# Two reordered parts, one later load, two wide zero products and one more split block in a vision tower kernel

## What is computed

```python
h = tok(x)                      # 768-long patches @ W_lin.T + b, class token, positions
h = h + attn(layernorm(h))      # 16 heads of 64, relative position bias, w_o
h = h + ffn(layernorm(h))       # below
h = h + recurrence(layernorm(h))
h = h + channel_mix(layernorm(h))

def ffn(x):                     # 592 tokens, hidden 1024
    logits = x @ router_w.T     # 7 routed experts, the best 2 of a token
    top_w = softmax(top_k(logits, 2))
    mixed = sum_e combine[:, e] * swiglu(x, w_gate[e], w_up[e], w_down[e])
    return mixed + swiglu(x, sw_gate, sw_up, sw_down)      # one shared expert
# swiglu(x) = (silu(x @ wg) * (x @ wu)) @ wd
```

## Time and profile before

| | |
|---|---|
| median of 3 runs | 306.15 us (306.04 to 307.07) |
| the profiled execution | 306.31 us |
| its span, first to last instruction | 304.5 us |
| PE busy | 296.6 us, 97% |
| ACT, DVE, POOL busy | 186.2, 188.9, 154.8 us |
| data moved | 46.49 MB, 153 GB/s |

### The profile page before, as it was taken

One profiled execution on the slowest core, in us unless ns is written; L12 is line 12 of the kernel. 1 busy time (PEld: TensorE's weight loads), 2 busy tenths in 40 slices (PEclk: granted clock), 3 DMA queues, 4 the chain that ended last, 5 costly groups with the idle time before them and its releaser, 6 DMA issues.

```text
span 304.5 us, 7355 instructions
## 1 busy us (share of the span) xinstructions
PE 296.6 (97%) x3072; PEld 276.6 (91%) x3072; DVE 188.9 (62%) x365; ACT 186.2 (61%) x324; POOL 154.8 (51%) x142
## 2 busy tenths in 40 slices
PE   8999999999999999989999999999999999998995
PEld 7778889998999999989999999999999999985673
DVE  1694446575727868665818784756648686736962
ACT  3486346766546884656777575657576563668561
POOL 7042624665415151829576694957685775000333
PEclk9999999999999999999999999999999999999999
DMA  7969444463504222477765848383857562000002
GB/s 257 409 165 231 88 116 135 139 187 102 166 10 145 77 107 84 163 219 272 250 196 186 244 130 272 102 297 111 276 169 257 188 191 66 11 2 2 1 0 84
DMA packets 32464, 46.49 MB, mean 153 GB/s; under 512 B 6997, under 2 KB 18869, under 8 KB 32426
## 3 DMA queue, kind: packets, MB, share of 16 engines
q1 hardware_dynamic: 30026, 42.16, 44.3%
q0 software_dynamic: 960, 2.43, 2.4%
q10 hardware_dynamic: 1440, 1.38, 1.5%
HBM read 38.22 MB, written 5.71 MB: 144 GB/s over the span
## 4 chain that ended last, share of the span: by engine, by line
PE 94%; DVE 3%; ACT 1%; issue 1%; ACTq 0%; POOL 0%; DVEq 0%; POOLq 0%
PE ps L1707 23%; PE ps L1709 22%; PE ps L1708 22%; PE ps L2098 6%; PE ps L1879 3%; PE ps L1722 3%; PE ps L1859 3%; PE ps L1729 2%; PE ps L1737 2%; PE ps L1844 2%; PE ps L1715 2%; PE ps L2007 1%; PE ps L1971 1%; ACT w_hi L853 1%; DVE xn_split L1477 1%
## 5 line engine op out<-in xcount | busy, mean ns | idle before, releaser
L1707 PE MATMUL ps<-c_region,w_hi 128*128 128x224 f32 (+2 forms) x300 | 86.8, 289 | 0.8 <-DVE c_region L1129 0.8
L1709 PE MATMUL ps<-c_region,w_lo 128*128 128x224 f32 (+2 forms) x300 | 84.2, 281 | 0.0
L1708 PE MATMUL ps<-c_region,w_hi 128*128 128x224 f32 (+2 forms) x300 | 84.0, 280 | 0.0
L572 POOL TENSOR_TENSOR w_lo<-w_stage,w_hi 128x512 fp32r<-128x512 f32 x30 | 47.4, 1603 | 33.3 <-ACT w_hi L847 33.3
L1707 PEld LDWEIGHTS ps<-c_region,w_hi 128*128 128x128 f32 x300 | 57.3, 191 | 1.6 <-DVE c_region L1129 1.1
L1708 PEld LDWEIGHTS ps<-c_region,w_hi 128*128 128x128 f32 x300 | 57.3, 191 | 0.3
L1709 PEld LDWEIGHTS ps<-c_region,w_lo 128*128 128x128 f32 x300 | 57.3, 191 | 0.0
L847 ACT ACTIVATE w_hi<-w_stage 128x1024 fp32r<-128x1024 f32 (+1 forms) x41 | 47.8, 1178 | 2.2 <-DVE v_region L1552 2.2
L1129 DVE TENSOR_TENSOR c_region<-s_region,c_region 128x448 fp32r<-128x448 f32 (+1 forms) x44 | 37.8, 861 | 15.2 <-ACT c_region L979 12.2
L579 POOL TENSOR_TENSOR w_lo<-w_stage,w_hi 128x512 fp32r<-128x512 f32 x26 | 35.2, 1387 | 8.9 <-ACT w_hi L847 7.3
L1707 PE MATMUL ps<-xn_split,w_hi 128*128 128x296 f32 x128 | 39.4, 308 | 0.0
(11 more groups left out here) (183 smaller groups left out, 566.5 us busy)
## 6 DMA issues: line engine op xcount, KB each, us to landing
w_stage<-in_w_gate SPq DMA_DIRECT2D x17, 512.0 KB, 5.0
w_stage<-in_w_up SPq DMA_DIRECT2D x17, 512.0 KB, 4.5
w_stage<-in_w_down SPq DMA_DIRECT2D x7, 1024.0 KB, 5.5
expert_rows<-blank_rows SPq DMA_DIRECT2D x4, 448.0 KB, 3.9
v_region<-in_blocks SPq DMA_DIRECT2D x6, 272.0 KB, 4.1
w_stage<-in_w_down SPq DMA_DIRECT2D x3, 512.0 KB, 4.9
v_region<-expert_rows SPq DMA_DIRECT2D x1, 1344.0 KB, 8.3
expert_out<-v_region ACTq DMA_DIRECT2D x6, 224.0 KB, 4.9
```

Of the source, the lines that this page charges most:

```text
L572: w = g.tensor_tensor(wl[:, r], ws[:, r], wh[:, r].bitcast(F32), ALU.subtract)
L1707: mm(o, a_h, b_h, start=start, stop=False)
L1708: mm(o, a_h, b_l, start=False, stop=False)
L1709: return mm(o, a_l, b_h, start=False, stop=stop)
```

## The change

- `FULL` goes from 3 to 2: block 2 of the patch product is split like blocks 3 to 5, in both halves. DVE gets one more `patch_low` behind `centre(0, 0)`.
- The head's six zero products of 128 x 128 become two of 512 columns, whose moving operand reads the zeros four times. A second call of `keep_clock`, late in the kernel, keeps its size.
- In half 1, PE does block 2 (now split) ahead of the variance and the bias product. Before, it did it there too, in full precision.
- SP issues the load of u1 behind the thirteenth key eviction, not behind the eleventh score tile.
- `shared_high(11)` comes ahead of `rows_high(1)` on ACT, `shared_low(11)` ahead of `rows_low(1)` on DVE.

```diff
-FULL = 3
+FULL = 2
@@ sync
             fill_rows(3)
-            sp.wait_ge(s["sc_ev"], 11)
+            sp.wait_ge(s["k_ev"], 13)
             load("u1", 0)
@@ scalar
+            shared_high(FRONT - 1)
             rows_high(1)
-            shared_high(FRONT - 1)
@@ vector
             patch_low(FULL + 2, 1, SPLIT0 + 3)
+            patch_low(FULL + 3, 1, SPLIT0 + 4)
             columns_low(2, 1, 1)
@@ vector
+            shared_low(FRONT - 1)
             rows_low(1)
-            shared_low(FRONT - 1)
@@ tensor
-                    mm(bank(b, cols)[0:cols, :], zero[:, 0:cols], zero[:, 0:cols], start=True, stop=True)
+                    mm(bank(b, cols), zero[:], pat(zero[:], 0, [0, cols // P], [1, P]), start=True, stop=True)
...
-            keep_clock(6)
+            keep_clock(2, cols=4 * P)
...
             mean(0, 0)
-            for k in range(1, FULL):
-                embed(k, 1)
-            variance(0, 0)
-            pe.wait_ge(s["d_bias_in"], 32)
-            mm(ps[0:HEADS, 5, 0:REL], tb[0:BUCKETS, :], cb[0:BUCKETS, CB_OH:CB_OH + REL],
-               start=True, stop=True).then_inc(s["bias_mm"], 1)
+            embed(1, 1)
             for k in range(FULL, KF):
                 pe.wait_ge(s["tok_lo"], 2 * (KF - FULL) + k - FULL + 1)
                 embed(k, 1)
+                if k == FULL:
+                    variance(0, 0)
+                    pe.wait_ge(s["d_bias_in"], 32)
+                    mm(ps[0:HEADS, 5, 0:REL], tb[0:BUCKETS, :], cb[0:BUCKETS, CB_OH:CB_OH + REL],
+                       start=True, stop=True).then_inc(s["bias_mm"], 1)
```

## The result

The changed kernel takes **305.17 us** (median of 9 runs, 304.72 to 305.57); the kernel before took 307.07 us beside it (9 runs, 306.04 to 309.26). The ratio is **0.9944**, with an interval of 0.9921 to 0.9966. The profiled execution took 305.05 us, with a span of 302.9 us (before: 306.31 and 304.5). So it is faster, by 1.3 us between the profiled executions (1.6 between their spans) where 1.9 was forecast, and the time lies inside the range of 303.5 to 305.7 us.

What follows compares the result with a forecast made beforehand. PE, busy 97% of the span, was taken to bound the kernel, so only its idle or excess work counted. From 306.31 us, +0.26 - 0.74 - 0.37 - 1.05 = -1.9 gave 304.4 us, range 303.5 to 305.7 us.

Steps and rivals of the forecast that it cites:

- u1: Attention, near 73.5 us: issuing u1 later lets the code load come sooner and removes an issue stall, -0.74 us.
- The rule on queue rows: DMA engines serve queue rows packet by packet, so the code load wouldn't wait and u1's edit would bring nothing.
- The slower rival: Attention: u1's packets delay the next code load, wanted from 73.0 us; +2.2 us, so 306.6 us; chance 0.06.
- the case that the prediction priced at nothing: Attention: the next code load slips in between u1 and `down` at 74.1 us, is there at 77.6, costs nothing.
- Where the blocks end: Attention, 68.08 us: eight fewer PE instructions ahead move the code block's end, so that issue stall goes, -0.37 us.
- End of the shared expert: Unit 11's parts, moved ahead of the gathered rows, end PE's wait before its `down`: -1.0 to -1.1 us, 1.05.
- the rival on their margin: End of shared expert: PE waits for the gathered rows instead, margin 0.23 us; 305.1 us at 0.7 us; chance 0.06.
- covered: First routed expert: POOL's two splits, ending at 139.40 and 144.85 us, are still in time for PE; no cost.
- its one assumption: Head: the clock rises at the same moment, 6.34 us, since PE streams without a gap from 0.98 us in both.
- +0.26: Head's total: wide zero products +0.43 us, block 2 split -0.17 us, if the clock rises at the same moment.
- the prediction's bound on the pass: Head: DVE's last split at 8.98 us keeps the first pass from ending before 9.78 us; at most -0.5 us.
- the rival of the earlier clock: Head: wide zero products raise the clock earlier, giving -0.5 instead of +0.26 us, so 303.6 us; chance 0.10.

Runs made afterwards that it cites:

- e1: Kernel before with only unit 11's high and low parts moved ahead of the gathered rows; 305.36 us, ratio 0.9963.
- e3: Kernel before with only the head's edits (block 2 split, two wide zero products); 305.76 us, ratio 0.9996.
- e6: Kernel before with four narrow zero products instead of six, eight instructions fewer; 307.56 us, ratio 1.0033.
- g1: Kernel before with eight narrow zero products instead of six, eight instructions more; 306.92 us, ratio 1.0015.
- e8: Changed kernel with the load of u1 back at its old wait; 308.02 us, ratio 0.9993.
- e2: Kernel before with only the load of u1 held back to the thirteenth key eviction; 305.54 us, ratio 0.9964.
- e4: Changed kernel run again with no edit, first group; 304.75 us, ratio 0.9955.
- f1: Changed kernel with the second gate ahead of DVE's low part in the first routed expert only; 304.42 us, ratio 0.9947.
- f2: Changed kernel with two narrow zero products in place of the two wide ones; 305.03 us, ratio 0.996.
- f3: f1 with one wide zero product in place of two; 307.24 us, ratio 0.9968, on a chip where all kernels were slower.
- e9: Changed kernel run a third time with no edit; 306.57 us, ratio 0.9943, on a chip where all kernels were slower.
- f4: f1 run again with no edit; 306.44 us, ratio 0.9946, on a chip where all kernels were slower.

## Why the prediction came out as it did

**u1: right, though the size of the stall varies.** The data packets of u1 held the load of code. With u1 early (before, e1, e3, e6, g1, e8) that load starts 2.9 to 4.3 us after the first product of the projection at 67.4 to 68.8 us, and PE stalls in all six; with u1 late (after, e2, e4, f1, f2, f3, e9, f4) it starts 1.3 to 2.3 us after it, and PE stalls in none of eight. The term was -0.74; by the signals it gave -0.77 in the first pair of profiles, and between e8 and e9 -1.27. The first profile of the kernel before had a mild case: the idle runs from 0.29 to 1.60 us among the six. Between the end of the load and PE's going on lie 1.2 to 1.4 us, close to the 1.2 us used. The prediction did not foresee that a long stall can be followed by a fall of the clock (e6_four). The rule on queue rows of the Trainium skill ("DMA: Bandwidth & Descriptors", queues, rings and completion order), by which the load would not have waited for a whole transfer, is not what these traces show. The slower rival, u1's packets ahead of the next load, came nowhere: that load started at 73.54 us, between u1 and `down`, and was in 1.4 us later, which is the case that the prediction priced at nothing.

**Where the blocks end: right.** -0.37 was taken, the bound of the cost in idle and first product; by the signals it was -0.47. The three alignments stand in a row: eight instructions more 0.95 us, none 0.47 (0.22 and 0.33 in e1 and e2), eight fewer nothing.

**End of the shared expert: right.** -1.05 forecast, -1.11 measured: the step to unit 11's `down` is 1.93 us in all five kernels without the edit and 0.81 or 0.82 in all nine with it. PE doesn't wait for the gathered rows in any of them, so the rival on their margin falls.

**What the sum left out: "covered".** That step failed. The prediction looked at whether POOL would be in time for PE, and it was. It didn't look at whom POOL's subtractions would lie beside once both engines' work moved by a microsecond by unequal amounts. DVE's low part took 1.1 us more, and through the second gate and ACT it cost PE 0.27 to 0.3 us. It comes with the reordered parts: the step is 5.6 us in the five kernels without them and 5.9 us in the six that have them and keep the gate's place. f1_gate_first shows most of the chain, since moving the gate alone gives 0.2 us back, in three kernels of three.

**The head: the working was right, its one assumption was not.** The forecast held that the clock would rise at the same moment. In eleven profiles without a gap ahead of block 0 the rise (by the trace's record of the granted clock, with which the spacing of the rows agrees to 0.2 us) lies anywhere from 4.2 to 7.1 us:

| kernel | zero products | rise, us | last product of the pass, us |
|---|---|---|---|
| before, e2 | narrow, 6 | 6.3, 6.2 | 10.16, 10.14 |
| e1, g1 | narrow, 6 and 8 | 4.5, 4.5 | 10.37, 10.12 |
| e8, e3, f1, after | wide, 2 | 4.2, 4.9, 5.0, 5.1 | 10.89, 10.40, 9.83, 10.11 |
| e4, f4, e9 | wide, 2 | 6.7, 6.8, 7.1 | 10.56, 10.66, 10.78 |
| f2, e6, f3 | gap of 1.36, 0.66, 0.56 us | 7.5, 8.7, 8.75 | 10.57, 11.43, 11.17 |

For a rise at time t the prediction's terms give 10.16 + 0.43 - 0.17 + (t - 6.34) / 2. For e4, f4 and e9 that is 10.58, 10.66 and 10.79 us, against 10.56, 10.66 and 10.78: so the +0.26 at an equal rise holds. With an early rise the feed decides, as the prediction's bound on the pass said: it can't give way before 9.78 us, and in f1, the earliest, the last product starts at 9.83 and gives way at 9.96 us. So the rival of the earlier clock came true in its condition and not in its price. In the first profile of after, PE waits for block 2's split, which DVE ends at 6.46 + 0.45 us, before its product of 6.97:

```profile
6.46 0.45 DVE L1129 TENSOR_TENSOR c_region<-v_region,c_region 128x288 fp32r<-128x288 f32 x1
```

In e8 the blocks themselves landed late: ACT takes up block 2 at 5.96 us and block 3 at 7.24 (5.67 and 6.40 in after), and PE stands 0.79 us before 7.26 us. Wide products don't bring the rise forward in these profiles: it comes at 4.5 to 6.3 us with narrow ones and at 4.2 to 7.1 with wide ones. So the head of the first pair, -0.05 in place of +0.26, was luck of 0.3 us, and it made up for the small wait that was left out.

**The sum.** Forecast +0.26 - 0.74 - 0.37 - 1.05 = -1.9 us. Measured -0.05 - 0.77 - 0.47 - 1.11 = -2.4, and then +0.61 at 131 us, +0.27 at 150 us and a tenth at the end make -1.4. The terms in question were all there and 0.5 us larger together; the two waits that no step foresaw took 0.9 us. Whether the kernel before would show the wait at 131 us on those chips is open: no profile of it was taken there. That the ratio is 0.9943 on the chip with that wait and 0.9955 on one without it speaks for yes, though the intervals overlap.

**The best version.** f1_gate_first has the lowest median (304.42 us), but beside the changed kernel it can't be told from it (306.44 and 306.57 us).

## What to carry to other kernels

PE's long unrolled program has block ends at fixed counts of instructions, and here the load of the next block came behind the data transfer that was issued just before it. A stall named "issue" with such a load landing ahead of it was mended by issuing the data some 2.5 us later. At the other place it was eight instructions fewer at the start of the program that did it, and eight more made it worse. When work moves by a microsecond, it is not enough to ask whether each engine is in time: look also at which VectorE and GpSimd instructions will now run beside each other, and put what others wait for ahead of the slow one. Zero products ahead of the first real one should last until its data land: the three kernels with a gap there had the latest rises. And no term of a few tenths that depends on the moment of the clock's rise is worth much from one profile.

## What the hardware showed that I had not expected

- The rise to 2.4 GHz comes at 4.2 to 7.1 us of the span in eleven profiles in which PE streamed from 0.98 us, and at 7.5 to 8.75 us in the three with 0.56 to 1.36 us of idle ahead of block 0. The three lie behind all eleven.
- One idle time of 1.60 us in attention, between small products, was followed by 3.4 us at 1.2 GHz, some 1.5 us lost behind the stall. Stalls of up to 1.05 us had no such sequel in the other profiles. Fourteen more executions, none traced, have the same low mean clock, all of kernels with u1 early.
- A DVE subtraction of two SBUF operands took 2.31 instead of 1.21 us, and POOL's pair 3.92 instead of 3.33 us, by a shift of 0.75 us of one against the other.
- Whole waits (0.6 us at 131 us, 0.6 to 1.3 us near 254 us) are there in all four kernels of one group and in none of the eight of the other two; the changed kernel, with no edit, is among both. PE's signals come up to 1.9 us late at the first of them, while its products run on.
